# Expert lists built from numbers in pairs, and the last layer norm in eight chunks

## What is computed

```python
    def _L0_ffn_ref(x, Wg, W1, b1, W2, b2):
        ...
        xt = x.reshape(n, h)                      # n = 4096 tokens, h = 256
        S = jax.nn.sigmoid(xt @ Wg).T             # 8 experts
        G, I = jax.lax.top_k(S, k)                # k = 1024 tokens for each expert
        ex = xt[I]
        hid = jax.nn.gelu(jnp.einsum('ekh,ehf->ekf', ex, W1) + b1[:, None, :], approximate=False)
        out = (jnp.einsum('ekf,efh->ekh', hid, W2) + b2[:, None, :]) * G[..., None]
        new_x = jnp.zeros_like(xt).at[I.reshape(-1)].add(out.reshape(-1, h))
        return new_x.reshape(b, l, h)
    ...
    x = _layernorm(x + _L0_ffn_ref(x, ...), axis=-1)
    return x
```

## Time and profile before

| | |
|---|---|
| median of 3 runs | 1446.86 us (1442.95 to 1447.52) |
| the profiled execution | 1447.94 us in all, of which the span is 1446.1 us |
| TensorE busy | 1104.2 us (76%) |
| VectorE busy | 1019.3 us (70%) |
| ScalarE busy | 748.1 us (52%) |
| GpSimd busy | 805.4 us (56%) |
| attention's last operation, then `choose_phase` | from 907.2 us |
| `expert_phase` | from 995.5 us |
| `final_phase` | 1407.1 to 1446.1 us |

### The profile page before, as it was taken

The page is one execution under the profiler, slowest core; times in us unless marked ns, Lnnn a source line. Parts: engine busy times, 40 slices in busy tenths (PEclk is TensorE's granted clock), DMA queues, the critical chain, the costliest instruction groups (busy, mean ns, idle before and its releaser), DMA issues. The chain is left out here.

```text
span 1446.1 us, 25901 instructions
## 1 busy us (share of the span) xinstructions
PE 1104.2 (76%) x8527; PEld 762.4 (53%) x8527; DVE 1019.3 (70%) x1875; ACT 748.1 (52%) x1605; POOL 805.4 (56%) x720
## 2 busy tenths in 40 slices
PE   5877778777787758888888886122999999999940
PEld 1322323222232237666676664022899899999940
DVE  2999999999999946677767765784455555555423
ACT  4666566575666436555666563100555555555425
POOL 2677676767768636666766764335144554455230
PEclk8999999999999979999999998555999999999975
DMA  3000000000000010111111100103134443343235
GB/s 103 15 15 1 15 0 15 15 0 15 0 0 0 1 28 27 35 33 33 33 41 36 33 32 26 65 1 101 56 63 107 94 106 81 89 112 55 24 47 215
DMA packets 42311, 64.00 MB, mean 44 GB/s; under 512 B 8161, under 2 KB 34465, under 8 KB 39073
## 3 DMA queue, kind: packets, MB, share of 16 engines
q1 hardware_dynamic: 29376, 41.92, 8.9%
q0 software_dynamic: 12288, 17.05, 7.2%
q10 hardware_dynamic: 576, 4.19, 0.7%
HBM read 42.00 MB, written 21.14 MB: 44 GB/s over the span
## 5 line engine op out<-in xcount | busy, mean ns | idle before, releaser
L514 POOL TENSOR_TENSOR scan_hc<-scan_state,scan_c_sb 128x1024 f32<-128x1024 f32 x128 | 304.1, 2380 | 142.9 <-DVE scan_state L442 132.0
L442 DVE TENSOR_TENSOR_SCAN scan_state<-scan_decay,scan_drive_ps 128x512 f32<-128x512 f32 x256 | 297.4, 1203 | 0.2
L223 PE MATMUL scan_y_ps<-scan_hc,all_ident 128*128 128x512 f32 x520 | 254.7, 613 | 2.1 <-POOL scan_hc L514 2.1
L1660 DVE TENSOR_TENSOR expert_hid_lo<-expert_hid,expert_hid_hi 128x512 fp32r<-128x512 f32 x128 | 88.5, 692 | 177.4 <-ACT expert_hid_hi L1644 165.7
L1557 POOL DMA_INDIRECT acc<-expert_rows,expert_lst x64 | 112.8, 1763 | 180.4 <-DVE expert_rows L1686 165.2
L1639 ACT ACTIVATE expert_hid<-expert_h_ps,expert_b 128x512 f32<-128x512 f32 x128 | 88.0, 688 | 200.0 <-PE expert_h_ps L556 191.9
L326 ACT ACTIVATE scan_decay<-scan_delta,scan_a_neg 128x508 f32<-128x508 f32 x256 | 169.2, 715 | 7.4 <-POOL scan_delta L496 7.2
L435 DVE TENSOR_TENSOR scan_drive_ps<-scan_dx,scan_b_ps 128x512 f32<-128x512 f32 x256 | 162.3, 679 | 14.6 <-POOL scan_dx L501 10.7
L368 ACT ACTIVATE scan_c_sb<-scan_c_ps 128x512 f32<-128x512 f32 x128 | 76.5, 598 | 138.2 <-PE scan_c_ps L216 129.2
L556 PE MATMUL expert_o_ps<-weights_w_hi,expert_hid_lo 128*128 128x256 f32 x512 | 143.4, 280 | 0.0
L554 PE MATMUL expert_o_ps<-weights_w_hi,expert_hid_hi 128*128 128x256 f32 x512 | 143.4, 280 | 0.0
(11 more groups left out here) (226 smaller groups left out, 2543.5 us busy)
## 6 DMA issues: line engine op xcount, KB each, us to landing
weights_w<-w SPq DMA_DIRECT2D x16, 1024.0 KB
table<-all_row SPq DMA_DIRECT2D x32, 132.0 KB, 1.8
scan_xT<-xT SPq DMA_DIRECT2D x8, 512.0 KB, 3.9
attn_ctxT<-ctxT SPq DMA_DIRECT2D x32, 128.0 KB, 2.4
acc<-all_row SPq DMA_DIRECT2D x32, 128.0 KB, 1.7
final_a<-acc SPq DMA_DIRECT2D x4, 1024.0 KB, 7.2
out<-final_o ACTq DMA_DIRECT2D x4, 1024.0 KB, 5.8
expert_b<-b SPq DMA_DIRECT2D x8, 128.0 KB
```

Of the source, the lines that this page charges most:

```text
L223: last = pe.matmul(y_ps[k][:], ident[0][:], hc[:, n % RING, k, :], start=False, stop=(n == NS - 1))
L442: dve.tensor_tensor_scan(state[:, n % RING, k, :], decay[:, n % RING, k, :, :].rearrange("p b t -> p (b t)"), drive_ps[k][:], 0.0, ALU.mul ...
L514: pool.tensor_tensor(hc[:, n % RING, :, :], state[:, n % RING, :, :], c_sb[:, n % RING, :].unsqueeze(1).broadcast_to([P, KH, GT]), ALU.mul ...
L1660: dve.tensor_tensor(hid_lo[:, f % RING_H, :], hid[:, f % 2, :], hid_hi[:, f % RING_H, :].bitcast(F32), ALU.subtract).then_inc(hid_ready, 1)
```

## The change

In the list building:

- `turned` and `tile_bf` hold every number twice, side by side. `tile_bf` is laid out in full for all 16 x 8 columns of a half.
- All comparisons and the products by the group's number read 32 numbers as 16 pairs: the innermost dimension is a pair with step 1, the one outside it repeats the pair 16 times. An instruction covers one half (`r`), 1024 numbers, so VectorE has six for a block instead of three of 2048.
- The products by the group's number go from GpSimd to VectorE, those by `place` from VectorE to ScalarE. GpSimd has nothing to do after the weights.

In the last phase:

- Eight chunks of 512 rows (0.5 MB), each with its own place in `a`, `o` and the small tensors; all loads are issued at once.
- Mean and variance come from `bn_aggr`, one small instruction for each row of a partition.
- Of four rows of a chunk ScalarE normalises two and GpSimd two; SP stores the chunk when both are done. VectorE takes the statistics of the next chunk ahead of the shift of this one.

```diff
-        tile_bf = s.sb("tile_bf", [P, 2 * CH], BF16)
+        tile_bf = s.sb("tile_bf", [P, 2, EXPERTS, CH, 2], BF16)
...
-        turned = s.sb("turned", [P, 2, M], BF16)
+        turned = s.sb("turned", [P, 2, M, 2], BF16)
...
+        def block_of(hot, b, r):
+            return hot[:, r * P + b * BLOCK:r * P + (b + 1) * BLOCK, :].rearrange("p m (l two) -> p m l two", two=2)
+
+        def over_pairs(row, b, r):
+            return row[:, r * P + b * BLOCK:r * P + (b + 1) * BLOCK, :].unsqueeze(2).broadcast_to([P, BLOCK, LO // 2, 2])
...
-                    pe.wait_ge(tile_ready, min(2 * (e // 2 + 1), EXPERTS - 1))
-                    if e == EXPERTS - 2:
-                        pe.wait_ge(last_tile_ready, 1)
+                    pe.wait_ge(tile_ready, e // 2 + 1)
...
-                pool.tensor_copy(tile_bf[:], place[:, 1:1 + 2 * CH]).then_inc(started, 1)
+                for r in range(2):
+                    last = pool.tensor_copy(tile_bf[:, r, :, :, :],
+                                            place[:, 1 + r * CH:1 + (r + 1) * CH].unsqueeze(1).unsqueeze(3).broadcast_to([P, EXPERTS, CH, 2]))
+                last.then_inc(started, 1)
...
-                for b in range(BLOCKS):
-                    pool.wait_ge(lo_ready, b + 1)
-                    times_tile(pool, b, 0, tile_ready)
-                    if b < BLOCKS - 1:
-                        times_tile(pool, b, 1, tile_ready)
...
+                for b in range(BLOCKS):
+                    act.wait_ge(lo_ready, b + 1)
+                    act.activation(lo_val[:].rearrange("p (r m) a l -> p r m a l", r=2)[:, :, b * BLOCK:(b + 1) * BLOCK, 0, :],
+                                   lo_hot[:].rearrange("p (r m) l -> p r m l", r=2)[:, :, b * BLOCK:(b + 1) * BLOCK, :],
+                                   ACT.Copy, scale=place[:, 0:1]).then_inc(place_ready, 1)
...
-                dve.tensor_copy(turned[:].rearrange("p h m -> p (h m)"), turn_ps[:]).then_inc(turned_ready, 1)
+                dve.tensor_copy(turned[:].rearrange("p h m two -> p (h m) two"),
+                                turn_ps[:].unsqueeze(2).broadcast_to([P, 2 * M, 2])).then_inc(turned_ready, 1)
...
-                        dve.tensor_tensor(hot[:].rearrange("p (r m) l -> p r m l", r=2)[:, :, cols, :],
-                                          turned[:, n, :].rearrange("p (r m) -> p r m", r=2)[:, :, cols].unsqueeze(3).broadcast_to([P, 2, BLOCK, LO]),
-                                          iota_bf[:].unsqueeze(1).unsqueeze(1).broadcast_to([P, 2, BLOCK, LO]), ALU.is_equal).then_inc(ready, 1)
+                        for r in range(2):
+                            last = dve.tensor_tensor(block_of(hot, b, r), over_pairs(turned[:, n, :, :], b, r),
+                                                     iota_bf[:].rearrange("p (l two) -> p l two", two=2).unsqueeze(1).broadcast_to([P, BLOCK, LO // 2, 2]),
+                                                     ALU.is_equal)
+                        last.then_inc(ready, 1)
                     dve.wait_ge(lo_ready, b + 1)
-                    dve.tensor_scalar(lo_val[:].rearrange("p (r m) a l -> p r m a l", r=2)[:, :, cols, 0, :],
-                                      lo_hot[:].rearrange("p (r m) l -> p r m l", r=2)[:, :, cols, :], place[:, 0:1], None, ALU.mult).then_inc(place_ready, 1)
-                    if b == BLOCKS - 1:
-                        times_tile(dve, b, 1, last_tile_ready)
+                    for r in range(2):
+                        last = dve.tensor_tensor(block_of(lo_val[:, :, 1, :], b, r), block_of(lo_hot, b, r),
+                                                 over_pairs(tile_bf[:].rearrange("p r e c two -> p (r e c) two"), b, r), ALU.mult)
+                    last.then_inc(tile_ready, 1)
```

The engines' lists in `final_phase` after the change (they replace the old ones as a whole):

```diff
+    C = 4
+    BY_POOL = 2
...
+                for c in range(CHUNKS):
+                    sp.dma_start(a[:, c, :, :], rows(acc_dram, c)).then_inc(loaded[c], 16)
+                for c in range(CHUNKS):
+                    sp.wait_ge(normed_act, c + 1)
+                    sp.wait_ge(normed_pool, c + 1)
+                    sp.dma_start(rows(out_dram, c), o[:, c, :, :]).then_inc(stored, 16)
+                sp.wait_ge(stored, 16 * CHUNKS)
...
+                def statistics(c):
+                    dve.wait_ge(loaded[c], 16)
+                    for t in range(C):
+                        last = dve.bn_stats(stats[:, c, t, :], a[:, c, t, :])
+                    last.then_inc(stats_ready, 1)
...
+                def aggregate(c):
+                    dve.wait_ge(stats_ready, c + 1)
+                    for t in range(C):
+                        last = dve.bn_aggr(moment[:, c, t, :], stats[:, c, t, :])
+                    last.then_inc(moments_ready, 1)
...
+                def shifts(c):
+                    dve.wait_ge(rstd_ready, c + 1)
+                    dve.scalar_tensor_tensor(shift[:, c, :], moment[:, c, :, 0], -1.0, rstd[:, c, :], ALU.mult, ALU.mult).then_inc(shift_ready, 1)
...
+                statistics(0)
+                for c in range(CHUNKS):
+                    aggregate(c)
+                    if c + 1 < CHUNKS:
+                        statistics(c + 1)
+                    shifts(c)
...
+                inv_std(0)
+                for c in range(CHUNKS):
+                    if c + 1 < CHUNKS:
+                        inv_std(c + 1)
+                    act.wait_ge(shift_ready, c + 1)
+                    for t in range(C - BY_POOL):
+                        last = act.activation(o[:, c, t, :], a[:, c, t, :], ACT.Identity, bias=shift[:, c, t:t + 1], scale=rstd[:, c, t:t + 1])
+                    last.then_inc(normed_act, 1)
...
+            @block.gpsimd
+            def _(pool):
+                for c in range(CHUNKS):
+                    pool.wait_ge(shift_ready, c + 1)
+                    for t in range(C - BY_POOL, C):
+                        last = pool.tensor_scalar(o[:, c, t, :], a[:, c, t, :], rstd[:, c, t:t + 1], shift[:, c, t:t + 1], ALU.mult, ALU.add)
+                    last.then_inc(normed_pool, 1)
```

More of the change, by code:

```diff
@@ L1711, in final_phase, with rows @@
 def final_phase(nc, acc_dram, out_dram):
-    C = 8
+    C = 4
     CHUNKS = T // (P * C)
+    BY_POOL = 2
     with ExitStack() as ctx:
         s = Scope(nc, ctx, "final")
-        a = [s.sb(f"a{i}", [P, C, D]) for i in range(2)]
-        o = [s.sb(f"o{i}", [P, C, D]) for i in range(2)]
-        stats = s.sb("stats", [P, C, 6])
-        part = s.sb("part", [P, 4, C])
-        mean = s.sb("mean", [P, C])
-        var = s.sb("var", [P, C])
-        lnv = s.sb("lnv", [P, C])
-        rstd = s.sb("rstd", [P, C])
-        shift = s.sb("shift", [P, C])
+        a = s.sb("a", [P, CHUNKS, C, D])
+        o = s.sb("o", [P, CHUNKS, C, D])
+        stats = s.sb("stats", [P, CHUNKS, C, 6])
+        moment = s.sb("moment", [P, CHUNKS, C, 2])
+        lnv = s.sb("lnv", [P, CHUNKS, C])
+        rstd = s.sb("rstd", [P, CHUNKS, C])
+        shift = s.sb("shift", [P, CHUNKS, C])
         eps = s.sb("eps", [P, 1])
-        shift_ready = s.sem("shift_ready")
-        loaded = [s.sem(f"loaded{i}") for i in range(2)]
-        stored = [s.sem(f"stored{i}") for i in range(2)]
+        loaded = [s.sem(f"loaded{c}") for c in range(CHUNKS)]
         stats_ready = s.sem("stats_ready")
-        moments = s.sem("moments")
+        moments_ready = s.sem("moments_ready")
         lnv_ready = s.sem("lnv_ready")
         rstd_ready = s.sem("rstd_ready")
-        normed = s.sem("normed")
+        shift_ready = s.sem("shift_ready")
+        normed_act = s.sem("normed_act")
+        normed_pool = s.sem("normed_pool")
+        stored = s.sem("stored")
         set_up = s.sem("set_up")
-        def both(eng, step):
-            step(0, 0)
-            step(0, 1)
-            with eng.Fori(1, CHUNKS // 2) as i:
-                step(i, 0)
-                step(i, 1)
+        def rows(dram, c):
+            return dram[c * P * C:(c + 1) * P * C, :].rearrange("(p t) d -> p t d", t=C)
         with nc.Block() as block:
@@ L1756, in _ @@
             @block.scalar
             def _(act):
-                def step(i, par):
-                    c = 2 * i + par
-                    act.wait_ge(moments, 3 * (c + 1))
-                    act.activation(lnv[:], var[:], ACT.Ln, bias=eps[:, 0:1]).then_inc(lnv_ready, 1)
-                    act.wait_ge(lnv_ready, c + 1)
-                    act.activation(rstd[:], lnv[:], ACT.Exp, scale=-0.5).then_inc(rstd_ready, 1)
-                    act.wait_ge(shift_ready, c + 1)
-                    since(act, stored[par], 16 * i)
-                    for t in range(C):
-                        last = act.activation(o[par][:, t, :], a[par][:, t, :], ACT.Identity, bias=shift[:, t:t + 1], scale=rstd[:, t:t + 1])
-                    last.then_inc(normed, 1)
-                    act.wait_ge(normed, c + 1)
-                    act.dma_start(out_dram[ds(c * P * C, P * C), :].rearrange("(p t) d -> p t d", t=C), o[par][:]).then_inc(stored[par], 16)
```

(22 more changed lines are left out.)

16 lines of the change are left out of this document (3 added, 13 removed).

## The result

The kernel with the change takes 1409.56 us (median of 4 runs, 1406.86 to 1413.79) beside 1446.04 (1442.95 to 1447.52): a ratio of 0.9753 [0.9723, 0.9783], 36.5 us faster.

What follows compares the result with a forecast made beforehand. VectorE was taken to bound the list building, no engine to be full in the last phase. From 1447.94 us, -19.8 (list) and -8.45 (last phase) gave 1419.7, less 1.1 to the median: 1418.6 us, range 1410 to 1426.

Steps and rivals of the forecast that it cites:

- VectorE's step in the list building: List building: each of VectorE's 24 instructions of 1024 numbers takes a step of 0.60 us, with 1.13 as upper bound.
- `turned` at double width: List building: writing 1024 numbers from PSUM instead of 512 costs VectorE 0.53 us more, so the first comparison starts later.
- `place` product on ScalarE: List building: one ScalarE instruction of 2048 numbers for a block takes at most 2.14 us.
- TensorE's last batch: End of list building: about 1.9 us at the full clock, between 1.8 and 3.57.
- tail to the store's issue: End of list building: list copied, token made and store issued, 1.25 us after TensorE's last batch.
- VectorE's chunk in the last phase: Last phase: four statistics, four aggregates and one shift take VectorE 1.72 us for a chunk.
- GpSimd's row: Last phase: each GpSimd `tensor_scalar` follows 1.18 us after the one before; 2.36 us a chunk makes GpSimd the bound.
- handover: Last phase: shifts end on GpSimd's instruction boundaries, then GpSimd waits for the semaphore, some 0.25 us a chunk.
- rival A: List building: pairs bring nothing, VectorE's step stays 1.13 us; gain 5.4, 1433.0 us in all; chance 0.09.
- B: List building: rows of two numbers cost VectorE time each, step 1.95 us; slower than before, 1452.7 us; chance 0.02.
- The rising clock: List building: with batches of 3.5 us every 3.6 us, TensorE reaches the full clock by the last batch.
- rival C: Last phase: GpSimd's `tensor_scalar` costs what its copies do, VectorE and DMA bound; gain 16.3, 1410.8 us; chance 0.10.

Runs made afterwards that it cites:

- e3: The changed kernel, but comparisons and products read one number 32 times again instead of pairs; 1421.6 us (0.9848).
- e5: The changed kernel, but GpSimd normalises its last-phase rows as (a - mean) * rstd instead of a * rstd + shift; 1415.69 us (0.9795).
- e11: The changed kernel with last-phase statistics of one row of four, ScalarE and GpSimd normalising one each, stores from the input tile; 1407.38 us in one run.
- e4: The changed kernel with pairs, but the products by the group's number go back to GpSimd; 1418.24 us (0.9823).

## Why the prediction was right for one half and wrong for the other

| | forecast | measured |
|---|---|---|
| VectorE's step in the list building | 0.60 us | 0.605 us (14.53 for 24) |
| `turned` at double width | +0.53 | +0.54 (1.23 against 0.69) |
| `place` product on ScalarE | at most 2.14 | 2.00 |
| TensorE's last batch | 1.9 | 2.03 |
| tail to the store's issue | 1.25 | 1.25 |
| the list part | -19.8 | -19.7 |
| VectorE's chunk in the last phase | 1.72 | 1.70 |
| GpSimd's row | 1.18 | 0.56 |
| handover | 0.25 a chunk | none to see |
| the last phase | -8.45 | -15.2 |
| unchanged phases | 0 | -3.8 in the profiles |

**The list building** came out as summed, no term off by more than 0.14 us. The choice that mattered was the step of 0.60 where the nearest row said 1.13. It was taken because the operand that makes the slow row slow was the one replaced, and `e3` shows exactly that. `e3` is rival A's list building made real, and its gain of 38.89 - 33.49 = 5.4 us is the one A was given. So A (1.13) and B (1.95) are out for the changed kernel. The rising clock came too: the last batch ran in 2.03 us, and in `e3`, with longer waits between batches, in 3.49.

**The last phase** failed first of all in the price of GpSimd's instruction, which the sum made the bound of the phase (2.36 us a chunk). The prediction took the earlier trace rows because form, size and types agreed, and noted in passing that the row subtracts where the change adds. That difference was the whole price: 1.22 against 0.56. `e5` shows that the rest of the working stood. With the dear form, and without the handover, it had given a gain of 10.2 us; measured in `e5` are 39.0 - 29.2 = 9.8.

With GpSimd at 1.1 us a chunk the phase went the way of rival C, given 0.10: VectorE's 1.70 and the DMA engines' bytes fill it, and its gain of 15.2 us is near C's 16.3. C had put GpSimd's row at the price of a copy, 0.40; it is 0.56, and only where nothing is subtracted. C's end of the span, 1.1 us behind the last byte, has no row, where the forecast took 0.4. Of C's two bounds, `e11` shows that the transfers alone are enough.

**The second failed term** is the handover, 1.75 us in all. Its reason was drawn from GpSimd instructions with two inputs, which hold VectorE up until they end (and 2.40 against 0.68 in `e4`). With one input they hold it only early on (three of seven shifts in `e5`, by 0.19 to 0.27 us), and GpSimd lost nothing by it. The Trainium skill (SBUF — State Buffer, "SBUF: two separate sides") has the port pair locked for a whole instruction whenever a VectorE instruction with two SBUF inputs meets a GpSimd one that reads SBUF. For two-input GpSimd work the runs agree up to the 0.58 us at a product's start in `e4`. For one-input work they don't: a lock held for whole instructions would have kept the shifts begun 0.86 us into one waiting for 0.35 us more, and they took 0.14.

From 1418.6 the last phase takes 6.8 us and the list gives back 0.1. That makes 1411.9, just inside the range that had been drawn for C (1410.8). Two things take it to 1409.56. The kernel before stands at 1446.04 in these runs and not at the 1446.86 that the sum started from, and the medians show 1.6 us more (36.5 - 34.9) outside the two stretches. The sum had neither, so how close the time came to the edge of the range is chance.

## What to carry to other kernels

Where a 16-bit operand is broadcast along the innermost dimension of a VectorE `tensor_tensor`, store the number twice and read pairs: it nearly halved the instruction here (0.68 instead of 1.21 us for 1024 numbers) for 0.54 us of a wider copy. Take a price only from a row with the same operations, not merely the same instruction name, size and types; on GpSimd write `a + (-m)` for `a - m`, and let a small instruction elsewhere make the negative. Once loads and stores fill the DMA engines in a window, read that window before the chain of waits: here the chain named VectorE, which was full too, and relieving it bought nothing.

## What the runs showed of the hardware that was not expected

- GpSimd's `tensor_scalar` on 256 float32 numbers in a partition: 0.55 to 0.56 us for the three pairs of additions and multiplications tried, 1.22 for the three pairs with a subtraction, 0.92 to 0.93 for one multiplication or subtraction alone.
- One-input GpSimd instructions of 1.20 us, run without a gap, delayed VectorE's two-input instructions by 0.27 us at most, and only those begun 0.15 to 0.22 us into one. Two-input ones of 2.3 us held a VectorE comparison until they ended and left it its 0.6 us at the next one's start; they themselves stayed undisturbed.
- The same instructions of the attention phase took between 382.5 and 387.9 us in different programs, and TensorE's busy time for the same matmuls went with it (313.1 to 319.4 us).
